# In the attention heads' loops, the scores for the row maxima are issued ahead of the scores by key

## What is computed

```python
x = x + _L0_attn_a_ref(_layernorm(x, axis=-1), ...)   # plain
x = x + _L0_ffn_ref(_layernorm(x, axis=-1), ...)
x = x + _L0_attn_b_ref(_layernorm(x, axis=-1), ...)
x = x + _L0_ffn_ref(_layernorm(x, axis=-1), ...)
x = x + _L1_attn_a_ref(_layernorm(x, axis=-1), ...)   # plain
x = x + _L1_ffn_ref(_layernorm(x, axis=-1), ...)
x = x + _L1_attn_b_ref(_layernorm(x, axis=-1), ...)   # latent
x = x + _L1_ffn_ref(_layernorm(x, axis=-1), ...)
```

```python
scores = (jnp.einsum('bhtd,bhsd->bhts', q, k) + jnp.einsum('bhtd,bsd->bhts', qr, kr)) * scale
causal = jnp.tril(jnp.ones((t, t), dtype=bool))
scores = jnp.where(causal[None, None], scores, jnp.float32(-jnp.inf))
attn = jax.nn.softmax(scores, axis=-1)
out = jnp.einsum('bhts,bhsd->bhtd', attn, v)
```

## Time and profile before

| | |
|---|---|
| timed runs | 1403.01, 1404.81, 1405.15 us, median 1404.81 |
| profiled execution | 1400.89 us, span 1399.1 us |
| granted TensorE clock, mean | 0.983 |
| busy TensorE, VectorE, ScalarE, GpSimd | 95%, 64%, 49%, 20% of the span |
| heads' loop of the first layer | about 50 to 227 us of the span |
| of the fifth layer | about 643 to 816 us |
| of the latent layer | about 1013 to 1241 us |

### The profile page before, as it was taken

The page is one execution under the profiler, slowest core; times in us unless marked ns, Lnnn a source line. Parts: engine busy times, 40 slices in busy tenths (PEclk is TensorE's granted clock), DMA queues, the critical chain, the costliest instruction groups (busy, mean ns, idle before and its releaser), DMA issues. The chain is left out here.

```text
span 1399.1 us, 33237 instructions
## 1 busy us (share of the span) xinstructions
PE 1330.8 (95%) x13909; PEld 747.2 (53%) x13917; DVE 894.1 (64%) x2163; ACT 690.6 (49%) x1043; POOL 278.2 (20%) x343
## 2 busy tenths in 40 slices
PE   8999999999679988999999999999899999999999
PEld 4455555475346774654555564436355555674436
DVE  5999994757486456759999835433655655536331
ACT  5578787636483226546777752111444444452110
POOL 5341522001420000053000000110533443210110
PEclk9999999999889999999999989999999999999999
DMA  4323300000300000032222030000300000000000
GB/s 96 69 40 68 72 3 31 5 2 1 121 1 4 17 1 16 1 59 40 38 36 37 8 114 0 1 0 7 65 14 16 17 14 15 9 2 1 0 0 30
DMA packets 33526, 37.50 MB, mean 27 GB/s; under 512 B 8722, under 2 KB 24194, under 8 KB 33378
## 3 DMA queue, kind: packets, MB, share of 16 engines
q1 hardware_dynamic: 33376, 35.38, 12.4%
q10 hardware_dynamic: 2, 0.00, 0.0%
HBM read 18.43 MB, written 1.07 MB: 14 GB/s over the span
## 5 line engine op out<-in xcount | busy, mean ns | idle before, releaser
L733 DVE TENSOR_REDUCE row_max_pieces<-psum 128x1 f32<-128x512 f32 (+3 forms) x672 | 407.1, 647 | 103.2 <-PE psum L615 101.3
L836 ACT ACTIVATE probs<-psum 128x1024 f32<-128x1024 f32 (+7 forms) x384 | 343.8, 901 | 199.6 <-PE psum L615 199.1
L674 PE MATMUL psum<-probs,v_ones 128*32 128x256 f32 (+1 forms) x2880 | 236.4, 362 | 8.8 <-POOL probs L604 4.4
L615 PE MATMUL psum<-q_all,k_head 97*32 97x512 f32 (+3 forms) x1536 | 177.1, 487 | 0.0
L615 PE MATMUL psum<-k_stack,q_stack 96*32 96x512 bf16 x2048 | 159.7, 379 | 3.4 <-issue 3.3
L615 PE MATMUL psum<-q_stack,k_stack 97*32 97x512 bf16 x2048 | 158.0, 379 | 2.0 <-issue 1.8
L674 PEld LDWEIGHTS psum<-probs,v_ones 128*32 128x32 f32 x2880 | 95.4, 109 | 87.9 <-POOL probs L604 24.3
L615 PEld LDWEIGHTS psum<-k_stack,q_stack 96*32 96x32 bf16 x2048 | 57.5, 95 | 65.8 <-DVE row_max_pieces L733 12.2
L615 PE MATMUL psum<-k_head_bf,q_all_bf 80*32 80x512 bf16 (+3 forms) x768 | 84.1, 328 | 3.2 <-ACT k_head_bf L2811 1.0
L615 PEld LDWEIGHTS psum<-q_stack,k_stack 97*32 97x32 bf16 x2048 | 58.4, 96 | 51.8 <-ACT probs L836 4.3
L615 PEld LDWEIGHTS psum<-q_all,k_head 97*32 97x32 f32 x1536 | 75.9, 109 | 18.0 <-issue 2.3
(11 more groups left out here) (402 smaller groups left out, 2078.3 us busy)
## 6 DMA issues: line engine op xcount, KB each, us to landing
q_stack<-arena SPq DMA_DIRECT2D x32, 96.0 KB, 2.7
k_stack<-arena SPq DMA_DIRECT2D x32, 96.0 KB, 3.0
arena<-gd_g_sums SPq DMA_DIRECT2D x6, 512.0 KB, 5.9
k_stack<-arena SPq DMA_DIRECT2D x32, 64.0 KB, 2.7
q_stack<-arena SPq DMA_DIRECT2D x32, 64.0 KB, 2.7
x_tokens<-in_x SPq DMA_DIRECT2D x4, 256.0 KB, 3.7
k_stack<-arena SPq DMA_DIRECT2D x32, 32.0 KB, 1.9
q_stack<-arena SPq DMA_DIRECT2D x32, 32.0 KB, 2.7
```

The source lines that it names most:

```text
L615: last = pe.matmul(o[j:j + 32], by[:, j:j + 32], rows, **flags)
L674: last = pe.matmul(psum[32 * g:32 * g + VW, PVB, first * P:end * P].rearrange("p (b n) -> p b n", n=P), V[:, c, h, :], by_group(pr[:, n % ...
L733: last = dve.reduce_max(mx[:, h % 2, qt, i:i + 1], o[:, 0:plain], AX.X)
L836: act.activation(pr[:, n % PB, q_from(c):], psum[:, 2 * (n % 2):2 * (n % 2) + 2, :].rearrange("p a n -> p (a n)")[:, q_from(c):], ACT.Exp, ...
```

## The change

In each iteration the call of `max_scores` moves ahead of that of `key_scores`. Nothing else is changed.

```diff
                 for n in range(CHUNKS):
-                    key_scores(n)
                     if n + LEAD < CHUNKS:
                         max_scores(n + LEAD)
+                    key_scores(n)
                     if n % NT == 3:
                         turn(n // NT + 1)
                     if rope and n % NT == rope.AT and n // NT + rope.AHEAD < HEADS:
                         rope_in(n // NT + rope.AHEAD)
                     if n >= LAG:
                         values(n - LAG)
```

## The result

| | before | after |
|---|---|---|
| timed runs | 1402.50 to 1405.15 us, 4 runs | 1420.22 to 1428.67 us, 4 runs |
| median | 1403.91 us | 1424.51 us |
| ratio, with its 95% interval | | 1.0148 (1.0123 to 1.0173) |
| profiled execution | 1400.89 us, span 1399.1 | 1428.67 us, span 1426.8 |
| granted TensorE clock, mean | 0.983 | 0.977 |

The kernel is 20.6 us slower (by the interval 17.3 to 24.3), and the forecast was 24.2 above the median of 1404.8 then known (1429).

A forecast was written before the change was run, and what follows sets the result against it. TensorE's queue was taken as the bound, where added waits lengthen the head. Plain-loop terms of 7.2 and 2.6 us plus 14.6 in the latent loop gave 24.4, which on the 1404.8 median made 1429; range 1412 to 1436.

The forecast's parts named there:

- The plain term: Plain attention loops: values of chunk 0 wait longer for ScalarE's copy; 7.2 us in ordinary heads, 2.6 in magnitude heads.
- the sum of nothing: Plain loops' start and end: maxima 0.43 us earlier, last exponentials 0.43 later, set at nothing; 0.4 per loop if one holds.
- The gap of VectorE: Magnitude heads of the plain loops: VectorE's 0.48 us gap should shrink, and it bounds nothing.
- The latent term: Latent loop, 12 heads with rotary work: 1.22 us more per head, 14.6 us in all.
- so the 1.03 passes through whole: Latent loop: the 1.03 us delay of chunk 7's key scores reaches the next head undiminished through ScalarE, GpSimd and the values.
- the wait at V(0): Latent loop: values of chunk 0 wait for ScalarE's copy of the finished head, adding 0.19 us per head.
- The lower bound: Latent loop: chunk 7's key scores delayed at least by 768 columns, 0.33 us in 12 heads, 4 us.
- the upper one: Latent loop: none of the 0.24 us counts as cover, 12 x (1.03 + 0.43) = 17.5 us.
- Only the plain loops: GpSimd's chain has slack in the latent loop, so only the plain loops lose 9.8 us: 1414.6; chance 0.14.
- only the latent loop: Plain loops hide their 0.36 us wait, so only the latent loop loses 14.6 us: 1419.4; chance 0.08.
- No change: Whole kernel: scores by key are never on the chain, time within 0.2% of 1404.8 us; chance 0.07.
- Rival (d): All loops: VectorE's ring ends last, earlier maxima remove TensorE's waits, 12.6 us faster, 1392; chance 0.06.

The follow-up runs named there:

- c = 1 alone: Scores for the maxima first only in the iteration on key chunk 1, in all three loops, against the kernel before: 1419.70 us, ratio 1.0128.
- c = 7 exempt: Latent loop alone, scores for the maxima first in every iteration but that on key chunk 7, against the kernel before: 1407.57 us, ratio 1.0038.
- the early `move_rope`: Changed kernel with ScalarE's copy for the rotary features one exponential earlier in the latent loop: 1412.91 us, ratio 1.0064 against the kernel before.
- the two halves: New order in the plain loops only, 1412.41 us, ratio 1.0078; in the latent loop only, 1414.75 us, ratio 1.009; each against the kernel before.

## Why the prediction was right, and where it was off

**The plain term** was right. The forecast chain of 2.10 us from KS(1) to V(0) with 1.74 of cover is what the trace of after shows, 0.36 in 12 successive heads, 13 waits in the fifth layer; in the magnitude heads 2.71 and 0.79. Moving the copy alone took it all away. It was forecast as 9.8 us and measured as 9.9 with the plain loops alone, 10.3 by that kernel's casts. That the first two numbers agree to 0.1 is luck, for a head was left out.

In head 14 the iteration c = 1 still has its MS; before the change V(0) waited 0.36 there behind four groups, after it behind three, so it waits 0.43 longer, in both loops. The timeline of TensorE at the turns of heads 13 and 14, after:

```profile
799.19 0.27 PE L641 MATMUL psum<-identity,minus_max 128*8 128x128 f32 x1
...
809.11 0.64 PE L674 MATMUL psum<-probs,v_ones 128*32 128x256 f32 x8 [0.61 <-ACT out_features L813]
...
810.11 0.27 PE L641 MATMUL psum<-identity,minus_max 128*8 128x128 f32 x1
```

810.11 - 799.19 = 10.92, where before it was 10.49. This 0.43 belongs to the end of the loops, which I had set at nothing, with 0.4 us per loop if only one side held; it makes 9.8 into 10.7, and the casts say 10.4 (5.4 and 5.0). At the start the sum of nothing held to 0.1 us: from the turn ahead of the loop to the first one in it (line 641, fifth layer) it is 11.06 us after the change and 11.33 before, and to the next one 11.31 against 10.78. That is 0.26 more in all, where one wait of 0.36 was counted.

**The gap of VectorE** in the magnitude heads was to shrink and grew, from 0.48 to 0.91 us. MS does follow V(0) at once, but V(0) itself is 0.43 later. It bounds nothing, as the prediction said.

**The latent term** was right in mechanism and too big: 1.22 forecast per head, 0.82 measured, 14.6 against 10.4 us by the casts. Step by step: the start of KS(7) is 0.99 us later behind the rotary product (3.22 against 2.23), where 1.03 was forecast. The step that failed is "so the 1.03 passes through whole". It doesn't, at its first link: the exponential is only 0.80 later. In the program an exponential waits for the last matmul of its KS, not for the first, and before the change KS(7) was drawn out: its pieces start between 1100.41 and 1100.76, mixed with the end of V(4) and the start of MS(5). After the change all its matmuls stand in one record at 1123.30 with the next work 0.22 behind, and the exponential follows the first of them by 0.47 instead of 0.66. From there on the 0.80 did pass through `move_rope` and GpSimd whole. The second step that failed is adding the wait at V(0). It is there, 0.19 or 0.20, as forecast, but 0.16 is given back from V(0) to the next rotary product, and the kernel with c = 1 alone shows that it costs 0.01 per head (14.89); what gives it back stays open. A third thing was not seen: KS(6) is late too, which shows only where KS(7) isn't the later of the two (0.24 with c = 7 exempt, 0.44 with the early `move_rope`). 12 x 0.82 is 9.8; the other 0.6 of the 10.4 is in the loop's first three distances. The lower bound (4 us) and the upper one (17.5) held it between them. With the latent term at 10.4 and the plain ones at 10.4 the sum is 20.8, so the forecast's 24.4 was 3.6 too high: 4.2 too much in the latent term, and 0.6 too little in the plain ones.

**The rivals.** Only the plain loops (1414.6) and only the latent loop (1419.4) are refuted by the two halves, each of which costs. No change, and faster, are refuted by the result. Rival (d) had a small part right: with `keep_out` early enough the plain heads are 10.95 to 10.98 apart instead of 11.00, because the turn follows its KS by 0.54 us instead of 0.57 (697.22 to 697.76 with the early copy, 798.62 to 799.19 in the timeline of after). So the 0.15 ahead of the turn isn't wholly fixed, as I had assumed; what takes 0.03 to 0.04 off it isn't shown. The gain is 0.5 us in 13 heads. The condition that I had set for it, the chain of 2.10 under 1.74, was the right one.

**The clock.** In the steady latent loop it stayed at 1.00, with waits of 0.9 us at V(6) in every head. The Trainium skill, TensorE: Matmul & The Clock Gate, section "A second HAM failure mode: psum-queue depth-cycling", describes a kernel that cycles its PSUM banks, idles briefly between groups and so drops and regains the clock; carried over to this loop it isn't borne out: the granted clock is 1.00 over 160 us. But the clock did fall at the start of that loop in the profiled execution, which no rival had. Three of the profiles show a first distance of the latent loop much above the 10.77 of before (14.37 after, 14.36 with all but c = 7, 12.64 with early `move_rope` in the changed kernel), and two with the same latent order as after don't (10.99 and 10.98). So it comes in some executions and not in others. Nor do the four with the old latent order and a lag of 2 (10.77 in each). Whether the new order makes it more frequent is open; one profile of each kernel can't tell. The medians agree with the sum of the distances without it, within the interval of 17.3 to 24.3, so nothing asks for it as a part of the 20.6.

## What to carry to other kernels

Moving equal work within an in-order queue changes nothing by its amount, but by the distance between a producer and the instruction that closes its chain. Measure the bare chain where the cover runs out (here the end of the loop) and compare it with the groups left in between; done so, the forecast for the plain loops was right to a hundredth of a microsecond per head. If an engine behind the moved instruction is the real limit, look for the line in *its* queue that can move earlier: here two lines of ScalarE's order, each tried alone on the changed kernel, took 14 us off the plain loops and 0.92 us off each of 12 latent heads, together more than the 20.6 that the change had cost (the two were not run together on it). And an experiment that moves only some iterations of a loop changes the spacing of the others' demands; it can bring a wait that neither full order has.

## What the hardware showed that I had not expected

- The clock at a stage's start differs from one execution to the next. At the latent layer's start it was 0.72 over 12 us and 0.79 over 16 in the profile of after, and 1.00 in that of before, where TensorE had waited 2 us less for a transfer. That the wait brought it on isn't shown: with the latent loop alone changed the clock is 0.83 from 990 to 1010 us with no wait for that transfer. The first head of the loop alone was 3.4 us longer than with the clock at 1.00 there (14.37 against 10.99).
- A ring wait can be invisible as idle time of the matmuls. In the kernel with c = 1 alone the matmul group shows as 0.72 long instead of 0.62, with no bracket, and the next start is 0.11 late; the reason stands only on the weight loads (PEld, waiting for VectorE).
- VectorE, busy 147.1 of 150 us, had no slack for uneven arrivals. With all chunks but 1 and 7 in the new order, two MS groups per head follow their predecessor after two groups instead of three, and three per head take 0.53 to 0.55 us instead of 0.434; their 0.31 is about the 0.28 by which the head grew.
